# Mamba stage of a two-layer decoder: GpSimd multiplies two chunks by C in one instruction, and its B tile is a scalar multiplication behind the second pair

## The reference

```python
xn = x * rsqrt(mean(x * x) + EPS) * g
x_s, z = split(xn @ W_in.T)                    # 512 inner features each
xc = silu(causal_conv4(x_s) + conv_b)
params = xc @ W_x.T                            # B (16), C (16), log dt (1)
dt = softplus(log_dt @ W_dt.T + b_dt)
A_bar = exp(dt[..., None] * A)
Bu = dt[..., None] * B[:, :, None, :] * xc[..., None]
h = A_bar * h + Bu                             # over the 256 tokens, 16 states
y = sum over states of h * C
out = x + ((y + xc * D) * silu(z)) @ W_out.T
```

## Time and profile before

| | us |
|---|---|
| median of 3 runs | 3867.53 |
| lowest, highest | 3866.7, 3871.18 |
| span of the profiled execution | 3867.2 |
| Mamba stage in that execution | about 1277 to 3086 |

### The profile page before, as it was taken

How to read it: one execution, slowest core, us unless ns; L and a number is a source line. 1 busy time by engine, 2 the same in 40 slices (tenths; PEclk the granted TensorE clock), 3 DMA queues, 4 the chain that set the end, 5 groups by cost and what they waited for, 6 DMA issues and landing times. The chain is left out here.

```text
span 3867.2 us, 75281 instructions
## 1 busy us (share of the span) xinstructions
PE 3312.9 (86%) x23360; PEld 2499.0 (65%) x23360; DVE 3139.9 (81%) x5227; ACT 2800.4 (72%) x5125; POOL 2652.0 (69%) x2858
## 2 busy tenths in 40 slices
PE   8996989889954789898898889888888879997887
PEld 5664666667532567776776767676766757775554
DVE  5665899945395899899899989989999859998886
ACT  2223787844475888888888888888888647776997
POOL 1222677720094799999898999989999836664666
PEclk9998999979976899999999999999999989998999
DMA  2111122251113111111111111111111112221111
GB/s 65 54 55 52 45 52 50 50 116 38 41 44 84 34 51 53 57 50 52 49 56 51 56 54 48 54 51 51 56 51 48 44 48 74 73 53 56 59 56 39
DMA packets 285550, 209.64 MB, mean 54 GB/s; under 512 B 131416, under 2 KB 249752, under 8 KB 285224
## 3 DMA queue, kind: packets, MB, share of 16 engines
q1 hardware_dynamic: 285224, 205.72, 19.0%
HBM read 149.18 MB, written 51.41 MB: 52 GB/s over the span
## 5 line engine op out<-in xcount | busy, mean ns | idle before, releaser
L2896 POOL TENSOR_TENSOR ma_ch<-ma_h,ma_crep 128x512 f32<-128x512 f32 x1024 | 1368.8, 1358 | 160.0 <-DVE ma_h L2998 147.5
L2998 DVE TENSOR_TENSOR_SCAN ma_h<-ma_a,ma_pbu 128x512 f32<-128x512 f32 x1024 | 1212.7, 1206 | 172.6 <-PE ma_pbu L2576 113.0
L2576 PE MATMUL ma_pbu<-ma_ident,ma_bu 128*128 128x128 f32 x4096 | 657.7, 285 | 203.1 <-DVE ma_h L2998 161.7
L2576 PEld LDWEIGHTS ma_pbu<-ma_ident,ma_bu 128*128 128x128 f32 x4096 | 478.9, 144 | 446.1 <-DVE ma_h L2998 317.5
L2783 ACT ACTIVATE ma_a<-ma_dt,ma_A 128x510 f32<-128x510 f32 x1024 | 653.5, 718 | 1.4 <-issue 1.4
L2585 PE MATMUL ma_py<-ma_ident,ma_ch 128*128 128x128 f32 x4096 | 625.0, 279 | 0.6 <-POOL ma_ch L2896 0.6
L2774 ACT ACTIVATE ma_bu<-ma_uT,ma_b_t 128x512 f32<-128x512 f32 x784 | 508.2, 719 | 14.4 <-PE ma_pbu L2576 12.2
L2585 PEld LDWEIGHTS ma_py<-ma_ident,ma_ch 128*128 128x128 f32 x4096 | 495.8, 145 | 0.9 <-POOL ma_ch L2896 0.8
L1576 POOL TENSOR_TENSOR xa_prob<-xa_e,xa_rec_head 128x616 f32<-128x616 f32 x128 | 155.5, 1216 | 126.7 <-DVE xa_rec_head L1668 114.7
L924 POOL TENSOR_TENSOR xa_prob<-xa_e,xa_rec_head 128x616 f32<-128x616 f32 x128 | 155.5, 1216 | 108.2 <-DVE xa_rec_head L1016 90.6
L362 POOL TENSOR_TENSOR la_veps<-la_mv,la_eps 128x2 f32<-128x2 f32 x32 | 6.2, 195 | 248.2 <-DVE la_mv L395 248.2
(11 more groups left out here) (373 smaller groups left out, 8041.2 us busy)
## 6 DMA issues: line engine op xcount, KB each, us to landing
ma_crep<-ma_ct_dram SPq DMA_DIRECT2D x256, 256.0 KB
xa_x<-act SPq DMA_DIRECT2D x64, 256.0 KB, 2.6
act<-xa_y SPq DMA_DIRECT2D x64, 256.0 KB, 2.2
la_x<-in_x SPq DMA_DIRECT2D x32, 256.0 KB, 2.7
act<-la_y SPq DMA_DIRECT2D x32, 256.0 KB
act<-ea_x SPq DMA_DIRECT2D x32, 256.0 KB, 4.0
ma_x<-act SPq DMA_DIRECT2D x16, 512.0 KB, 4.5
ma_xr<-act SPq DMA_DIRECT2D x16, 512.0 KB
```

The costliest lines, as they stand in the source:

```text
L2576: last = pe.transpose(pbu[c % 2][:, t * P:(t + 1) * P], bu[:, s % 2, t, c * P:(c + 1) * P], ident[:, :])
L2896: pool.tensor_tensor(ch[:, s % 2, c], h[:, s % 2, c], crep[:, s % 4, :], ALU.mult).then_inc(multiplied, 1)
L2998: dve.tensor_tensor_scan(out=h[:, s % 2, c, :], data0=a[:, s % 2, c, :], data1=pbu[c % 2][:, :], initial=0.0, op0=ALU.mult, op1=ALU.add).t ...
```

## The change

`times_c` handles two chunks (c, c + 1) in one instruction of 128 x 2 x 512, with C broadcast over the two; it waits for the second chunk's scan and for the sum of the second chunk eight earlier, and adds 2 to `multiplied`. The bu tile of POOL is written as a `tensor_scalar` with two multiplications, by the column of B and by 1.0, instead of a `tensor_tensor` with B's column broadcast. It comes behind the second pair of state s and is for state s + 2, no longer behind (s,0) for s + 1, and its waits are taken ahead of that pair. The other steps of POOL keep their places behind the pair that holds their chunk; `rms_of` so moves from behind (5,2) to behind (5,3). The numbers of `multiplied`, `summed` and `pool_tile_ready` that other engines wait for are unchanged.

```diff
--- before.py
+++ after.py
@@ -2888,20 +2888,24 @@
                 pool.tensor_tensor(rdiag[:, :, :], ident[:, :].unsqueeze(1).broadcast_to([P, TT, P]),
                                    rms[:, :].unsqueeze(2).broadcast_to([P, TT, P]), ALU.mult).then_inc(rdiag_ready, 1)
 
-            def times_c(g, s, c):
-                pool.wait_ge(scanned, K * g + (IC * s + c + 9))
-                if c == 0:
+            def times_c(g, s, pair):
+                c = 2 * pair
+                pool.wait_ge(scanned, K * g + (IC * s + c + 10))
+                if pair == 0:
                     pool.wait_ge(c_loaded[s % 4], (4 * 16) * g + 16 * (s // 4 + 1))
-                pool.wait_ge(summed, K * g + (IC * s + c + 1))
-                pool.tensor_tensor(ch[:, s % 2, c], h[:, s % 2, c], crep[:, s % 4, :], ALU.mult).then_inc(multiplied, 1)
-
-            def scale_tile(g, par, s):
+                pool.wait_ge(summed, K * g + (IC * s + c + 2))
+                pool.tensor_tensor(ch[:, s % 2, c:c + 2], h[:, s % 2, c:c + 2],
+                                   crep[:, s % 4, :].unsqueeze(1).broadcast_to([P, 2, GS]), ALU.mult).then_inc(multiplied, 2)
+
+            def tile_may_be_scaled(g, s):
                 pool.wait_ge(uT_copied, IC * g + IC)
                 pool.wait_ge(b_copied, g + 1)
                 pool.wait_ge(bu_turned, K * g + (IC * s + 4))
+
+            def scale_tile(g, par, s):
                 t = TT - 1 - DVE_TILES.get(s, 0)
-                pool.tensor_tensor(bu[:, s % 2, t, :], uT[:, par, t, :],
-                                   b_t[:, par, t, s:s + 1].broadcast_to([P, DI]), ALU.mult).then_inc(pool_tile_ready, 1)
+                pool.tensor_scalar(bu[:, s % 2, t, :], uT[:, par, t, :], b_t[:, par, t, s:s + 1], 1.0,
+                                   ALU.mult, ALU.mult).then_inc(pool_tile_ready, 1)
 
             def step_input(n, par, c):
                 pool.wait_ge(rest_ready, IC * n + (c + 1))
@@ -2913,23 +2917,23 @@
                 link(pool.tensor_tensor(veps[:, k], mv[:, k, 1], eps5[:, k], ALU.add))
                 pool.tensor_tensor(rstd[:, k], veps[:, k], minus_half[:, k], ALU.pow).then_inc(rstd_ready, 1)
 
-            INPUTS = {(11, 1): 0, (11, 3): 1, (12, 1): 2, (12, 3): 3}
-
             def group(g, par, first, last):
                 n, prep = g + 1, not last
                 ahead = not (type(g) is int and g + 2 >= NG)
                 for s in range(N):
-                    for c in range(IC):
-                        times_c(g, s, c)
-                        if c == 0 and s + 1 in POOL_TILES:
-                            scale_tile(g, par, s + 1)
-                        if prep and (s, c) in INPUTS:
-                            step_input(n, 1 - par, INPUTS[s, c])
-                        if (s, c) in ((6, 1), (10, 3)) and not first:
+                    for pair in range(IC // 2):
+                        if pair == 1 and s + 2 in POOL_TILES:
+                            tile_may_be_scaled(g, s + 2)
+                        times_c(g, s, pair)
+                        if pair == 1 and s + 2 in POOL_TILES:
+                            scale_tile(g, par, s + 2)
+                        if prep and s in (11, 12):
+                            step_input(n, 1 - par, 2 * (s - 11) + pair)
+                        if (s, pair) in ((6, 0), (10, 1)) and not first:
                             rstd_of(g - 1, 0 if s == 6 else 1)
-                        if s == 5 and c == 2 and ahead:
+                        if s == 5 and pair == 1 and ahead:
                             rms_of(g + 2)
-                        if s == 6 and c == 3 and ahead:
+                        if s == 6 and pair == 1 and ahead:
                             rms_diagonal(g + 2)
 
             pool.memset(eps6[:, :], 1e-6 * D)
```

## The result

The changed kernel takes **3956.0 us** (median of 5 runs, 3954.54 to 3963.12) against 3867.53: a ratio of 1.0226, interval 1.0215 to 1.0237. It is slower by 88.5 us, where 85.8 had been forecast, and inside the range of 3862 to 4000. In the profiled execution the span grew by 86.0 us. First the page's first line; then the busy times of the Mamba stage, with the columns of the earlier trace rows.

What follows compares the result with a forecast made beforehand. It took DVE in the Mamba stage as the bound, with little waiting for POOL. Terms of 5.0 + 0.5 + 0.5 + 0.5 - 0.75 = 5.75 us a group, times 15, gave 86 on 3867.2: 3953 us, range 3862 to 4000.

Steps and rivals of the forecast that it cites:

- Longer holds: DVE's SBUF-only operations wait for whole pairs on POOL: 7.7 us a group late in the group, 5.0 more than before.
- signs: Marks of a right forecast: L2992 and L2988 lengths near 1.9 us, L3008's mean above 1.1, pairs near 2.4.
- Products: On POOL, 64 products a group become 32 of 2.37 us, saving about 0.13 us a pair, 4 us a group.
- their lateness: A first chunk's product comes a scan later; PE sums a chunk six turns on, so costed at nothing.
- Tile: POOL's bu tile in scalar form, 8 a group: 1.53 us each instead of 1.04, giving back the pairs' 4 us.
- Place of the tile: POOL's tile behind pair (s,1) for s + 2: PE's 11.4 us of waiting should go, 0.75 us a group.
- one_plus and the tile behind (9,0): DVE operations meeting POOL's longer instructions: 0.5 us a group for the two one_plus, 0.5 for the tile.
- The four tiles behind (6,0) to (8,0): DVE's tiles there wait longer, hidden by idle time before (8,0) and (9,0); uncovered, up to 1.2 us each.
- a pair lets DVE in between its rows: Rival: DVE gets in between a pair's two rows of 512, holds stay as now: 3856 us, chance 0.12.
- POOL as the bound: Rival: POOL's back-up paces the Mamba stage, so 4.2 us a group come back: 3805 us, chance 0.05.
- absorption by the scans' idle time: Rival: DVE's longer waits are taken from 172.6 us of idle time behind them: 3867 us, no change, chance 0.08.
- the slow tile: Rival: POOL's tile takes 2.3 us, 6 us more work a group and longer holds: 3980 us, chance 0.10.

Runs made afterwards that it cites:

- e2: Changed kernel with POOL's tile again a two-input product with B's column broadcast, in its new place, pairs kept: 3967.35 us, 1.0267 against the kernel before.
- e1: Changed kernel with single products and one-chunk waits again, only the tile's new form and place kept: 3863.35 us, 0.9987 against the kernel before.
- e7: Changed kernel, pairs whole, with rstd_of put ahead of the pair of its chunk: 3967.31 us, 1.0252 against the kernel before.
- e9: Changed kernel with pairs in states 1 to 5 alone, single products elsewhere: 3862.26 us, 0.9983 against the kernel before.
- e6: e3 with rstd_of put ahead of the pair of its chunk: 3894.96 us, 1.0062 against the kernel before.
- e8: e7 with DVE's SBUF-only operations behind odd scans, take_lost and u merged to 1024 elements: 3885.84 us, 1.0039 against the kernel before.
- e3: Changed kernel with each pair issued as two products back to back, same waits and order: 3889.77 us, 1.0058 against the kernel before.

## Why the prediction was right

**The mechanism was right, and so was the number, in part by luck.** From the starts of the scans, in the mean of the 12 middle groups, a group grew from 114.62 to 120.03 us, by 5.41 against a predicted 5.75. By stretch:

| chunks | predicted, us a group | measured |
|---|---|---|
| (0,0) to (1,3) | +0.5 | +0.63 |
| (2,0) to (7,3) | -0.75, put on no place | -0.27 |
| (8,0) to (11,0) | 0.5 + 0.5 + 1.16 = +2.16 | +1.54 |
| (11,1) to (15,3) | 5.0 - 1.16 = +3.84 | +3.51 |

The luck: the sum counted 15 groups, and these grew by 82 us in place of 86. The last one, which prepares no other and was put at nothing, grew by 5.4 us too and made up for it.

**Longer holds** was right to about 0.1 us a wait for most, at worst 0.17. Predicted, less 0.07 each: 1.16, 0.37, 0.07, 1.16, 1.30, 0.07, 1.16, 1.30, 0, 1.16, or 7.7. In the group of the timelines: 1.06, 0.47, 0, 1.05, 1.47, 0, 1.06, 1.34, 0, 1.01, or 7.5. As signs, the means were named too high: L3008's was to pass 1.1 us and reached 0.956, and of the four L2992 only two were long, so their mean rose from 1229 to 1260 ns alone.

The exclusive lock of SBUF — State Buffer of the Trainium skill, section "Who interferes with whom", by which the prediction said its sum stands, is borne out for an instruction of two rows: the gT of 2563.64 waited 1.47 us and ended 0.55 us behind the pair. The split products show what only a run could: two instructions in a row give DVE its turn between them (the av of 2415.40).

**Products** was right: 2372 ns against 2374. So was putting their lateness at nothing: scans, PE and its weight loads wait 4.9 us for products in all, where it was 12.7 before.

**Tile** was wrong, in the step that took the scalar row (1.224 us for 256 elements) as the nearest: 700 ns were measured for 512. That instruction subtracts and multiplies by two columns, this one multiplies by one column and by 1.0; the row was of the same operation and another form. GPSIMD Engine Reference of the Trainium skill, section 3.1, with its 769 ns was the better guide, 10% above the measured 700. The miss moved the forecast little: by the prediction's own estimate, a tile of 0.77 lowers the sum by some 5 us. e2 says what a slow tile does cost: 344 ns more on 128 tiles, 11 us.

**Place of the tile** gave less than was put down. PE's wait of 11.4 us went, but e1 gained only 5 us from that and the faster form together: its scans wait 125.9 us for PE against 113.0, so part of the time was only waited for elsewhere.

**one_plus and the tile behind (9,0)** were put at 0.5 us a group each. `one_plus` rose from 1307 to 1367 ns, 0.12 a group; the bu tile behind (9,0) took 0.55 us in the group of the timelines, 0.1 over its shortest. So of the 2.16 of the third stretch the gT behind (11,0) came nearly as forecast (1.06 of 1.16), these two brought some 0.2 in place of 1.0, and the rest of the measured 1.54 is mostly idle time before scans, 0.4 us a group more in the middle groups.

**The four tiles behind (6,0) to (8,0)** were to wait longer under cover of idle time. They did not wait longer at all: in the middle groups they take 3.4 us together, as against 3.5 before.

**What was overlooked:** rstd behind pair (6,0) is 1.05 us late for `finish` before (7,0), 16.8 us in all. The prediction had no term for it. The stretch from (2,0) to (7,3) shows that this cost next to nothing, and e7 that taking it away gains nothing.

**The rivals.** That a pair lets DVE in between its rows is ruled out by the timelines, POOL as the bound by the windows (POOL is busy 142 us less and the kernel is slower), absorption by the scans' idle time, which gave back only 13.4 us, and the slow tile by its 700 ns.

## What to carry to other kernels

Before making an engine's instructions fewer and longer, look at which other engine is held off while one of them runs: here joining two products saved 0.18 us (twice 1278 ns against 2372) on an engine that little waited for, and nearly doubled the time, 2.37 us in place of 1.28, for which one product holds off DVE's SBUF-only operations. A mean far above the shortest time in a group of instructions, with no idle before it, is how such a hold looks in a profile; following the two queues from one scan's end gave the waits of the longer hold within a few per cent (7.7 against 7.5 us). Join instructions only over stretches where the other engine's work reads PSUM (e9, and even there nothing was gained that can be told), and do not expect the wait to vanish when one obstacle is moved (e6, e7, e8).

## What the runs showed that was not expected

The hold works in both directions. The prediction's walk had let POOL's rstd stand behind a DVE operation; what the trace adds is how long POOL's instructions become by it. POOL's step input, which the change did not touch, as min/median/max, in the kernel before and then in the changed one:

```profile
L2908 POOL TENSOR_TENSOR ma_dt<-ma_dt,ma_gT x64: 1258/1716/2278, 1261.1 to 2974.9; 128x512 f32<-128x512 f32 x64
```

```profile
L2912 POOL TENSOR_TENSOR ma_dt<-ma_dt,ma_gT x64: 1642/1713/2240, 1257.9 to 3050.4; 128x512 f32<-128x512 f32 x64
```

Before, some took 1.26 us; now none takes less than 1.64, though the median stayed. The timeline shows one: the pair ends at 2565.22, the gT that had waited for it ends at 2565.77, and the step input of 2565.18 takes 1.72 us, 0.46 more than the shortest of before. The second product of e3 shown above, 1.71 us in place of 1.27, is another. DVE goes first, and POOL stands meanwhile. So in these two a hold costs DVE the rest of the POOL instruction, and then POOL most of the DVE operation.

And one scalar instruction on POOL is not like another: 700 ns for 512 elements with one column and a constant, 1224 for 256 with two columns.
